# Moving the odd tokens by one partition: a TensorE matmul and a ScalarE copy in place of SyncE's DMAs

## The chip, the cores and the metric

One core of a Trainium2 chip runs the whole program. The metric is the device time of one execution in microseconds, the median of several runs. The profile is taken from one execution, and its times are counted from the start of its span.

## What is computed

A metaformer block on x of shape (4, 64, 32, 32). First a layer norm over channels, a deformable 3x3 convolution (offsets and masks from another 3x3 convolution, four corners gathered for each tap), batch norm, SiLU, and the residual sum. Then a token mixer over T = 1024 tokens of 64 channels: a layer norm of each token, K = 16 causal filters of full length, two mixing matrices for each filter, and a short autoregressive part of three lags; the weighted sum of four branches, each on a prefix of the tokens.

```
x = x + _L0_conv_ref(_ln_c(x), ...)
t = _to_tokens(x)
t = t + _L0_ffn_ref(_ln_t(t), ...)      # _stu of four prefixes, weighted
...
U_plus = irfft(Vf * rfft(u)); U_minus = irfft(Vf * rfft(u * sgn)) * sgn
out = einsum('btkd,k,kde->bte', U_plus, s, Mpp) + einsum('btkd,k,kde->bte', U_minus, s, Mpm)
```

U_plus and U_minus together are convolutions between tokens of even and of odd place, so the kernel keeps the two apart.

## The kernel before

The four images go as two pairs (bp = 0, 1). A pair's 1024 tokens are cut into NJ = 4 units of 128 even and 128 odd tokens, so there are NQ = 8 units, each with one pass n = 0 to 7; bp, j = divmod(n, 4). Tokens lie on partitions in reverse order.

VectorE makes the tokens. For each unit q and parity p it waits for the gathered corners, weighs them (weigh(q, p, b2): L459, L460, and L463, which writes V), TensorE transposes V (turn_values, L838 and L839) and convolves it (convolve_values, L848; turn_convolved), ScalarE takes the exponential (L654), and VectorE activates and normalises (finish(q, p), from L471), ending with two writes to u16 at L493 and L494 which raise u_ready. u16[:, q, hl, b, w, c] holds in slot w = 1 the even and in slot w = 0 the odd tokens as a high and a low f16 part (hl), for two images b.

Its order in time is: weigh(q, 1, 0), weigh(q, 1, 1), positions and weights of unit q + 2, finish(q, 0), weigh(q+1, 0, 0), finish(q, 1), weigh(q+1, 0, 1), and on to q + 1. V has one buffer for each image (b2), so a V write waits until TensorE's turn_values has read the last one. POOL issues the gathers, nine (one a tap) for each of the four (p, b2) of a unit, into one buffer each (L279).

TensorE runs pass n as 16 steps k. convolve(i) multiplies the filters of group i // 4 with tokens: par = i % 2 picks slots 0 and 1 or slots 1 and 2 of u16, and the result goes to conv_ps[par], one PSUM bank each. It does 3 matmuls for each unit j2 = 0 to j of the pair; only the last three, j2 = j, need the new unit. ScalarE copies each result out (L680, two copies). After convolve(k) come, each at its own k, turn_pass(n - 1) (k = 1, L876), turn_tokens(2n + 1) (k = 3, L859), turn_values for the next unit (k = 3 and 11), convolve_values (4 and 12), turn_convolved (5 and 13), turn_tokens(2n + 2) (k = 10, L859, which needs the even tokens of unit n + 1), and from k = 4 the mixing of an earlier filter (mix, L919).

Slot 2 of u16 has to hold the odd tokens moved by one partition: partition s takes slot 0 of partition s + 1, and the last partition takes partition 0 of the unit before (zero for the first unit of a pair). Before the change SyncE does this with DMAs from SBUF to SBUF, L257 for 127 partitions and L259 for the last one, 14 in all. TensorE waits for them in convolve(1) ahead of its last three matmuls (L899).

Of the kernel before, what the change touches and what calls it, by code (L numbers as in the profile page):

```python
# [5 lines left out]
F32, F16, I32 = mybir.dt.float32, mybir.dt.float16, mybir.dt.int32  # L6
ALU, ACT, AX = mybir.AluOpType, mybir.ActivationFunctionType, mybir.AxisListType

P = 128
B, C, H, W = 4, 64, 32, 32  # L10
T = H * W
BP = B // 2
NJ = T // (2 * P)
NQ = BP * NJ
# [12 lines left out]
STEPS = 4 * N_GROUPS  # L27
# [5 lines left out]
START = 2  # L33
# [14 lines left out]
def metaformer_kernel(nc, x, offset_w, offset_b, mask_w, mask_b, weight, gamma, beta, mean, var,  # L48
                      sigma, phi, m_u, m_plus, m_minus, log_weights, gumbel, ident_in, grid_in, first_row_in, out):
    ctx = ExitStack()  # L50
    with ctx:
        def sb(name, shape, dt=F32):
            return ctx.enter_context(nc.sbuf_tensor(name, shape, dt))

        def sem(name):
            return ctx.enter_context(nc.semaphore(name))
# [14 lines left out]
        ident, swap = ident_swap[:, 0, :], ident_swap[:, 1, :]  # L71
# [3 lines left out]
        zeros = sb("zeros", [C, 2 * C])  # L75
        ones = sb("ones", [K, P])
        off_bias = sb("off_bias", [P, NOFF])
        w_off = sb("w_off", [P, TAPS, NCH])
        w_scaled = sb("w_scaled", [C, TAPS * C])
        w_main = sb("w_main", [P, 5, C])  # L80
# [26 lines left out]
        u16 = sb("u16", [P, NQ, 2, 2, 3, C], F16)  # L107
# [74 lines left out]
        filt_loaded = [sem(f"filt_loaded{k}") for k in range(K)]  # L182
        conv_done = [sem(f"conv_done{i}") for i in range(2)]
        conv_copied = [sem(f"conv_copied{i}") for i in range(2)]
        shift_zeroed, u_shifted, mix_scaled = sem("shift_zeroed"), sem("u_shifted"), sem("mix_scaled")
        group_mixed, mixed_copied, pass_turned = sem("group_mixed"), sem("mixed_copied"), sem("pass_turned")
        out_copied, out_stored = sem("out_copied"), [sem(f"out_stored{i}") for i in range(2)]
        dve_step = sem("dve_step")
# [19 lines left out]
        @block.sync  # L208
        def _(sp):
            sp.dma_start(x_ch[:, 0, :], ap(x, 0, [[T, P], [1, T]])).then_inc(s_x[0], 16)  # L210
            sp.dma_start(ident_swap[:], ident_in).then_inc(s_ident, 16)
            sp.dma_start(w_off_raw[0:2 * TAPS, :], ap(offset_w, 0, [[C * TAPS, 2 * TAPS], [1, C * TAPS]])).then_inc(s_woff, 16)
            sp.dma_start(w_off_raw[2 * TAPS:NOFF, :], ap(mask_w, 0, [[C * TAPS, TAPS], [1, C * TAPS]])).then_inc(s_woff, 16)
            sp.dma_start(grid[:], grid_in).then_inc(s_const, 16)
            sp.dma_start(first_row[:], first_row_in).then_inc(s_const, 16)
            sp.dma_start(off_bias[:, 0:2 * TAPS], ap(offset_b, 0, [[0, P], [1, 2 * TAPS]])).then_inc(s_const, 16)
            sp.dma_start(off_bias[:, 2 * TAPS:NOFF], ap(mask_b, 0, [[0, P], [1, TAPS]])).then_inc(s_const, 16)
            sp.dma_start(phi_sb, ap(phi, 0, [[2 * K, P], [2 * P * K, NJ], [1, 2 * K]]).rearrange("s j (p k) -> s j p k", p=2)
                         ).then_inc(s_phi, 16)
            sp.dma_start(x_ch[:, 1, :], ap(x, 2 * C * T, [[T, P], [1, T]])).then_inc(s_x[1], 16)  # L220

            sp.wait_ge(zeroed, 1)
            for bp in range(BP):
                for first in (2 * C, 2 * C * (1 + H * W) + C):
                    sp.dma_start(ap(table[bp], first, [[IMAGE * 2 * C, 2], [2 * C, W], [1, C]]), zeros[:, 0:C]
                                 ).then_inc(border_stored, 16)
                sp.dma_start(ap(table[bp], 0, [[IMAGE * 2 * C, 3], [1, 2 * C]]), zeros[0:3, :]).then_inc(border_stored, 16)
            load_matrices(sp, 0, m_plus, range(BRANCHES))
            store_image(sp, 0, 0, 0)
            store_image(sp, 0, 1, 0)  # L230
            load_matrices(sp, 1, m_minus, range(2, BRANCHES))
            for r in range(BRANCHES):
                sp.dma_start(mu_raw[:, r, :].rearrange("d (i e) -> d i e", i=3),
                             ap(m_u, r * 3 * C * C, [[C, C], [C * C, 3], [1, C]])).then_inc(s_mats, 16)
            sp.wait_ge(f_rows_ready, 1)
            sp.dma_start(ap(hankel, 0, [[4 * HROW, K], [1, 4 * HROW]]), f_rows.rearrange("k p h c -> k (p h c)")
                         ).then_inc(f_rows_stored, 16)
            for b2 in range(2):
                for cy in range(2):
                    store_image(sp, 1, b2, cy)  # L240

            def load_filters(ks):
                for k in ks:
                    sp.dma_start(filt_h[:, k].rearrange("s p h c -> s (p h) c"),
                                 ap(hankel, k * 4 * HROW + HPAD - 2 - (P - 1), [[1, P], [HROW, 4], [1, HLEN]])
                                 ).then_inc(filt_loaded[k], 16)

            sp.wait_ge(f_rows_stored, 16)
            load_filters(range(8))
            sp.wait_ge(mats_summed, 2 * BRANCHES)  # L250
            sp.wait_ge(off_turned, 2 * BP)
            sp.wait_ge(w_ready, 2)
            load_filters(range(8, K))
            sp.wait_ge(shift_zeroed, BP)
            for q in range(NQ):
                sp.wait_ge(u_ready, 2 * q + 2)
                sp.dma_start(u16[0:P - 1, q, :, :, 2], u16[1:P, q, :, :, 0]).then_inc(u_shifted, 16)  # L257
                if q % NJ:
                    sp.dma_start(u16[P - 1:P, q, :, :, 2], u16[0:1, q - 1, :, :, 0]).then_inc(u_shifted, 16)  # L259

        @block.gpsimd
        def _(pool):
# [22 lines left out]
        def _(dve):  # L285
# [19 lines left out]
            dve.memset(ones[:], 1.0).then_inc(ones_ready, 1)  # L305
            dve.memset(roots[:, 0, 0:C], 1.0).then_inc(roots_set, 1)
            dve.memset(f_rows, 0.0)
            for q in range(0, NQ, NJ):
                dve.memset(u16[3 * P // 4:P, q, :, :, 2], 0.0).then_inc(shift_zeroed, 1)

            def reverse_pixels(bp):
                dve.wait_ge(s_x[bp], 16)
# [1 line left out]

            reverse_pixels(0)

            dve.wait_ge(s_woff, 32)
            raw = w_off_raw.rearrange("o (c t) -> o t c", t=TAPS)
            dve.tensor_copy(w_off_dup[:, :, 0, :], raw)
# [243 lines left out]
        def _(act):  # L563
# [119 lines left out]
            def store_pass(n):  # L683

                act.wait_ge(pass_turned, n + 1)
                if n >= 2:
# [4 lines left out]
                act.dma_start(ap(out, (n // NJ) * 2 * C * T + 2 * P * (n % NJ), [[T, P], [1, 2 * P]]),  # L691
                              o_sb[:, n % 2, :]).then_inc(out_stored[n % 2], 16)

            for n in range(NQ):
                for k in range(K):
                    copy_products(n, k)
                    if k == ODD_TOKENS_AT:
                        copy_tokens(2 * n + 1)
                    if n and k == 1:
                        store_pass(n - 1)  # L700
                    if n == NQ - 1:
                        continue
                    for p, (values_at, y_at, turn_at) in enumerate(HOSTED_AT):
                        r = 2 * n + 2 + p
                        if k == values_at:
                            copy_values(r)
                        if k == y_at:
                            copy_convolved(r)
                        if k == turn_at:
                            exp_y(r)  # L710
                    if k == TOKENS_AT:
                        copy_tokens(2 * n + 2)
                act.wait_ge(group_mixed, N_GROUPS * (n + 1))
                act.copy(mixed[:], acc_ps[n % 2][:, 0:2 * P].rearrange("e (b a) -> e b a", b=2)).then_inc(mixed_copied, 1)
# [5 lines left out]
        def _(pe):  # L720
# [139 lines left out]

            pe.wait_ge(w_copied, 1)
            pe.wait_ge(ones_ready, 2)
            for r in range(2):
                turn_values(r)
                convolve_values(r)
                turn_convolved(r)
# [13 lines left out]
            for n in range(NQ):  # L880
# [4 lines left out]
                ranges = [(s, max(SEGS[s][0], P * j) - P * j, min(SEGS[s][1], P * j + P) - P * j)  # L885
                          for s in range(seg0, seg0 + nseg)]

                def convolve(i):

                    g, b2, par = i // 4, i // 2 % 2, i % 2  # L890
                    if n == 0 and i % 4 == 0:
                        for k in range(GROUP * g, GROUP * g + GROUP):
                            pe.wait_ge(filt_loaded[k], 16)
                    pe.wait_ge(conv_copied[par], START + STEPS * n + 2 * (i // 2))
                    for j2 in range(j + 1):
                        if j2 == j and i == 0:
                            pe.wait_ge(u_ready, 2 * n + 2)
                        if j2 == j and i == 1:
                            pe.wait_ge(u_shifted, 16 * (7 * bp + 2 * j + 1))  # L899
                        lag = P * (j - j2)  # L900
                        for e, (hl, part) in enumerate(((0, 0), (0, 1), (1, 0))):
                            last = pe.matmul(conv_ps[par][:].rearrange("c (k a) -> c k a", k=GROUP),  # L902
                                             u16[:, NJ * bp + j2, hl, b2, par:par + 2].rearrange("s w c -> s (w c)"),
                                             filt_h[:, GROUP * g:GROUP * g + GROUP, par, part, lag + 2:lag + 2 + P],
                                             start=(j2 == 0 and e == 0), stop=(j2 == j and e == 2))
                    last.then_inc(conv_done[par], 1)
# [110 lines left out]
```

## Time and profile before

| | |
|---|---|
| median of 3 runs | 545.5 us (543.98 to 546.7) |
| the profiled execution | 545.57 us, span 543.4 us |
| mean granted clock of TensorE | 0.899 |
| PE busy | 439.2 us, 81% |
| VectorE busy | 316.9 us, 58% |
| ScalarE busy | 206.4 us, 38% |
| POOL busy | 296.8 us, 55% |

The difference of some 2 us between an execution's time and its span lies around the profiled work. Busy shares are means over the start (until about 110 us), in which filters, matrices and the first tokens are made, and the eight passes of TensorE, which follow one another to the end.

### The profile page before, as it was taken

The numbers are of one execution on the slowest core, as the hardware profiler recorded it, in microseconds if no ns is written. First come the engines' busy times: TensorE is split into PE (matmuls) and PEld (weight loads), VectorE is DVE, ScalarE is ACT, GpSimd is POOL, SyncE is SP. The second block draws the span as 40 slices with busy tenths as digits, with TensorE's granted clock in tenths as the row PEclk, the third lists the DMA queues.
The fourth block names the chain that finished last, engine by engine and source line by source line (L and its number), as shares of the span: only waits on it lengthen the run. The fifth ranks groups of instructions, "written<-read, shape, count | busy, mean of one in ns | idle before, by whom it ended". The sixth has DMA issues, their size and how long they took to land.

```text
span 543.4 us, 7147 instructions
## 1 busy us (share of the span) xinstructions
PE 439.2 (81%) x2660; PEld 217.9 (40%) x2660; DVE 316.9 (58%) x768; ACT 206.4 (38%) x413; POOL 296.8 (55%) x295
## 2 busy tenths in 40 slices
PE   4986481438775995999989996976699699989997
PEld 3442441315443442444434342643344354534333
DVE  5759977999864959292738429677374934040000
ACT  2124120125543562434333343654356244424232
POOL 1067777778777777777777773777776000000000
PEclk9999595558897999799989998889699889999999
DMA  6943699832334333333333332333433000000000
GB/s 154 185 109 106 155 326 349 259 111 83 102 102 112 102 98 109 103 104 103 104 109 98 104 100 53 104 93 108 114 103 97 6 10 1 2 5 11 0 1 10
DMA packets 47746, 54.41 MB, mean 100 GB/s; under 512 B 28656, under 2 KB 38134, under 8 KB 47713
## 3 DMA queue, kind: packets, MB, share of 16 engines
q0 software_dynamic: 13824, 37.77, 23.6%
q1 hardware_dynamic: 27865, 13.94, 10.2%
q10 hardware_dynamic: 6024, 2.26, 1.9%
q8 instruction: 21, 0.34, 0.3%
q14 instruction: 12, 0.10, 0.1%
HBM read 50.12 MB, written 3.30 MB: 98 GB/s over the span
## 4 chain that ended last, share of the span: by engine, by line
PE 58%; DVE 24%; DMA 10%; issue 3%; ACT 2%; SPq 1%; DVEq 0%
PE bank L902 32%; DMA u<-u 9%; PE bank L919 7%; PE bank L848 3%; PE bank L779 3%; DVE G L459 3%; PE bank L838 3%; DVE sil L472 2%; PE bank L760 2%; DVE G L460 2%; PE bank L939 2%; PE bank L876 1%; DMA filt<-in_L_ffn_phi_dram 1%; DVE V L463 1%; DVE st L299 1%
## 5 line engine op out<-in xcount | busy, mean ns | idle before, releaser
L279 POOL DMA_INDIRECT G<-corner_table,idx x288 | 294.2, 1022 | 122.0 <-issue 86.2
L902 PE MATMUL bank<-filt,u 128*128 128x512 f16 x960 | 243.2, 397 | 46.5 <-DMA u<-u 38.4
L680 ACT COPY u_conv<-bank 64x512 f32<-64x512 f32 x256 | 148.3, 579 | 202.7 <-PE bank L902 198.7
L902 PEld LDWEIGHTS bank<-filt,u 128*128 128x128 f16 x960 | 89.5, 100 | 167.8 <-issue 49.9
L919 PE MATMUL bank<-u_conv,mixw 128*64 128x256 f32 (+1 forms) x640 | 79.2, 356 | 5.9 <-issue 5.9
L459 DVE TENSOR_TENSOR G<-G,bank 128x2304 f32<-128x2304 f32 x32 | 81.5, 2547 | 1.3 <-DMA G<-corner_table,idx 1.2
L463 DVE TENSOR_TENSOR V<-G 128x576 f32<-128x576 f32 x32 | 24.4, 761 | 67.9 <-PE bank L839 67.2
L919 PEld LDWEIGHTS bank<-u_conv,mixw 128*64 128x64 f32 x640 | 35.8, 137 | 52.1 <-issue 50.6
L460 DVE TENSOR_TENSOR G<-G 128x1152 f32<-128x1152 f32 x32 | 43.5, 1358 | 1.1
L471 DVE TENSOR_SCALAR expo<-expo 128x128 f32<-128x128 f32 x16 | 4.4, 274 | 59.4 <-ACT expo L654 59.1
L838 PE MATMUL bank<-ident_swap,V 128*128 128x128 f32 x128 | 22.3, 309 | 14.6 <-DVE V L463 12.1
L644 ACT COPY vT<-bank 128x512 f32<-128x512 f32 x32 | 17.2, 592 | 25.5 <-PE bank L839 25.4
L848 PE MATMUL bank<-vT,w_main 128*64 128x128 f32 (+1 forms) x320 | 22.6, 292 | 3.6 <-ACT vT L645 3.6
L838 PEld LDWEIGHTS bank<-ident_swap,V 128*128 128x128 f32 x128 | 17.1, 160 | 17.8 <-issue 17.6
L848 PEld LDWEIGHTS bank<-vT,w_main 128*64 128x64 f32 (+1 forms) x320 | 20.2, 148 | 6.3 <-issue 4.9
L760 PE MATMUL bank<-ident_swap,n_uT 128*64 128x128 f32 x64 | 10.7, 361 | 12.1 <-DVE n_uT L343 12.1
L779 PE MATMUL bank<-filt,w_off 64*32 64x512 f32 x144 | 18.1, 646 | 0.0
L600 ACT COPY filt<-bank 64x256 f32<-64x256 f32 x16 | 5.4, 394 | 27.0 <-PE bank L760 27.0
L472 DVE RECIPROCAL sil<-expo 128x128 f32<-128x128 f32 x16 | 15.2, 953 | 0.5
L760 PEld LDWEIGHTS bank<-ident_swap,n_uT 128*64 128x64 f32 x64 | 10.0, 192 | 13.0 <-DVE n_uT L343 12.4
L859 PE MATMUL bank<-ident_swap,u_tok 128*128 128x128 f32 x32 | 7.4, 316 | 6.4 <-DVE u L494 6.4
L939 PE MATMUL bank<-n_uT,mu 64*64 64x256 f32 (+1 forms) x120 | 12.2, 339 | 0.0
(153 smaller groups left out, 308.5 us busy)
## 6 DMA issues: line engine op xcount, KB each, us to landing
filt<-filter_rows SPq DMA_DIRECT2D x16, 514.0 KB, 12.2
G<-corner_table,idx POOLq DMA_INDIRECT x288
corner_table<-n_uT SPq DMA_DIRECT2D x12, 128.0 KB, 3.5
mixw<-in_x_dram SPq DMA_DIRECT2D x2, 512.0 KB, 6.3
filt<-in_L_ffn_M_phi_plus_dram SPq DMA_DIRECT2D x4, 256.0 KB, 7.5
out_dram<-o_sb ACTq DMA_DIRECT2D x8, 128.0 KB, 2.0
filt<-n_L_ffn_M_phi_minus_dram ACTq DMA_DIRECT2D x2, 256.0 KB, 5.6
corner_table<-n_uT ACTq DMA_DIRECT2D x4, 128.0 KB, 4.8
```

Of the source, the lines that this page charges most:

```text
L279: pool.indirect_dma_start(G[:, k, tap, :], None, corners[bp], bass.IndirectOffsetOnAxis(ap=idx[:, q % 2, k, tap:tap + 1], axis=0)).then_in ...
L459: link(dve.tensor_tensor(g, g, w, ALU.mult))
L460: link(dve.tensor_tensor(G[:, k, :, 0:2 * C], G[:, k, :, 0:2 * C], G[:, k, :, 2 * C:4 * C], ALU.add))
L463: dve.tensor_tensor(V[:, b2].rearrange("s (t c) -> s t c", c=C), G[:, k, :, 0:C], G[:, k, :, C:2 * C], ALU.add).then_inc(v_ready[b2], 1)
L472: link(dve.reciprocal(sil[:], expo[:]))
L680: act.copy(u_conv[C * par:C * par + C, g % 2, :, b2, p, :], conv_ps[par][rows].rearrange("c (k a) -> c k a", k=GROUP)).then_inc(conv_copie ...
L760: last = pe.matmul(bank[2 + jj][C * b2:C * b2 + C, 256 * p + P * (1 - j2):256 * p + P * (1 - j2) + P], n_tok[:, NJ * bp + NJ - 1 - 2 * jj ...
L779: last = pe.matmul(bank[b2][group:group + NCH, :], w_off[half, tap, :], a, start=(t == 0), stop=(tap == TAP_HALVES[tg][-1]))
L838: pe.transpose(val_ps[b2][:, P * m:P * m + P], V[:, b2, P * m:P * m + P], ident)
L848: last = pe.matmul(y_chan_ps[C * b2:C * b2 + C, :], w_main[0:rows, m, :], vT[0:rows, b2, m, :], start=(m == 0), stop=(m == 4))
L902: last = pe.matmul(conv_ps[par][:].rearrange("c (k a) -> c k a", k=GROUP), u16[:, NJ * bp + j2, hl, b2, par:par + 2].rearrange("s w c -> s ...
L919: last = pe.matmul(acc[C * p:C * p + C, 0:2 * P].rearrange("e (b a) -> e b a", b=2)[:, :, a0:a1], mixw[:, s, C * k:C * k + C], u_conv[:, g ...
```

## The change

The DMAs and the memsets of slot 2 go. VectorE writes a "ladder" of 128 x 256 in f16 at the start: the identity with zeros left and right of it. In each pass TensorE multiplies slot 0 of the new unit by a slice of the ladder that moves it by one partition, and, for j > 0, adds partition 0 of the unit before by a second matmul. The result goes to conv_ps[1], of which ScalarE copies 256 columns to slot 2. convolve(1) waits for this copy ahead of its first matmul.

```diff
+        ladder = sb("ladder", [P, 2 * P], F16)
...
-            sp.wait_ge(shift_zeroed, BP)
-            for q in range(NQ):
-                sp.wait_ge(u_ready, 2 * q + 2)
-                sp.dma_start(u16[0:P - 1, q, :, :, 2], u16[1:P, q, :, :, 0]).then_inc(u_shifted, 16)
-                if q % NJ:
-                    sp.dma_start(u16[P - 1:P, q, :, :, 2], u16[0:1, q - 1, :, :, 0]).then_inc(u_shifted, 16)
...
-            for q in range(0, NQ, NJ):
-                dve.memset(u16[3 * P // 4:P, q, :, :, 2], 0.0).then_inc(shift_zeroed, 1)
+            dve.memset(ladder[:, 0:P - 1], 0.0)
+            dve.memset(ladder[:, 2 * P - 1:2 * P], 0.0)
...
+            dve.wait_ge(s_ident, 16)
+            dve.tensor_copy(ladder[:, P - 1:2 * P - 1], ident).then_inc(ladder_ready, 1)
...
+            def copy_stepped(n):
+
+                act.wait_ge(u_stepped, n + 1)
+                act.copy(u16[:, n, :, :, 2], conv_ps[1][:, 0:4 * C].rearrange("s (h b c) -> s h b c", h=2, b=2)).then_inc(u_shifted, 1)
+
             for n in range(NQ):
+                copy_stepped(n)
                 for k in range(K):
                     copy_products(n, k)
...
+            pe.wait_ge(ladder_ready, 1)
...
+                def step_odd_tokens():
+
+                    pe.wait_ge(u_ready, 2 * n + 2)
+                    pe.wait_ge(conv_copied[1], START + STEPS * n)
+                    dst = conv_ps[1][:, 0:4 * C].rearrange("s (h b c) -> s h b c", h=2, b=2)
+                    last = pe.matmul(dst, ladder[:, P:2 * P], u16[:, n, :, :, 0], start=True, stop=(j == 0))
+                    if j:
+                        last = pe.matmul(dst, ladder[:, 0:P], u16[:, n - 1, :, :, 0], start=False, stop=True)
+                    last.then_inc(u_stepped, 1)
+
...
                     for j2 in range(j + 1):
                         if j2 == j and i == 0:
-                            pe.wait_ge(u_ready, 2 * n + 2)
-                        if j2 == j and i == 1:
-                            pe.wait_ge(u_shifted, 16 * (7 * bp + 2 * j + 1))
+                            step_odd_tokens()
+                        if j2 == 0 and i == 1:
+                            pe.wait_ge(u_shifted, n + 1)
```

## Rows read from the trace of the kernel before

**Rows 1.** The page: shares of the chain that ended last, and the convolution's group.

```profile
PE bank L902 32%; DMA u<-u 9%; PE bank L919 7%; PE bank L848 3%; PE bank L779 3%; DVE G L459 3%; PE bank L838 3%; DVE sil L472 2%; PE bank L760 2%; DVE G L460 2%; PE bank L939 2%; PE bank L876 1%; DMA filt<-in_L_ffn_phi_dram 1%; DVE V L463 1%; DVE st L299 1%
...
L902 PE MATMUL bank<-filt,u 128*128 128x512 f16 x960 | 243.2, 397 | 46.5 <-DMA u<-u 38.4
```

**Rows 2.** The waits: engine and line, whom for, us in total, times, longest.

```profile
POOL G L279 <- DVE V L463: 9.1, 4, 7.8
```

**Rows 3.** Timeline of TensorE, pass 2: start, us, work, [idle before <- releaser].

```profile
208.37 3.43 PE L902 MATMUL bank<-filt,u 128*128 128x512 f16 x15
217.87 1.46 PE L902 MATMUL bank<-filt,u 128*128 128x512 f16 x3 [6.08 <-DMA u<-u]
219.26 1.12 PE L876 MATMUL bank<-mixed,ident_swap 128*64 128x128 f32 x8
220.32 5.58 PE L902 MATMUL bank<-filt,u 128*128 128x512 f16 x18
```

**Rows 4.** Windows: pass 0; then first matmul or tokens to k = 3, passes 1-3, 5-7.

```profile
core 0: us, PE busy (x) PEld busy (x) DVE busy (x) ACT busy (x) POOL busy (x), PEclk, DMA share, GB/s
110.18:143.60 33.42, 20.68 (x148) 10.98 (x148) 31.66 (x73) 14.89 (x28) 26.11 (x25) 0.79 0.33 98
160.12:174.34 14.22, 6.96 (x29) 2.87 (x30) 8.43 (x5) 3.78 (x7) 11.17 (x11) 0.76 0.40 111
208.37:225.73 17.36, 11.28 (x46) 4.59 (x44) 9.07 (x8) 4.02 (x8) 13.40 (x14) 0.80 0.38 109
267.58:282.91 15.33, 12.67 (x58) 5.39 (x56) 7.80 (x5) 4.02 (x8) 11.98 (x12) 0.89 0.39 108
376.28:391.56 15.28, 8.16 (x30) 3.16 (x30) 8.34 (x5) 3.87 (x7) 11.93 (x12) 0.66 0.42 112
425.58:440.71 15.13, 11.34 (x46) 4.58 (x44) 8.91 (x7) 4.02 (x8) 0.00 (x0) 0.77 0.06 14
482.56:495.03 12.47, 11.30 (x59) 4.95 (x56) 0.00 (x0) 4.02 (x8) 0.00 (x0) 1.00 0.06 16
```

**Rows 5.** Timeline of TensorE, pass 7, after its wait.

```profile
488.45 0.82 PE L902 MATMUL bank<-filt,u 128*128 128x512 f16 x3 [1.17 <-DMA u<-u]
489.21 0.66 PE L876 MATMUL bank<-mixed,ident_swap 128*64 128x128 f32 x8
489.80 5.39 PE L902 MATMUL bank<-filt,u 128*128 128x512 f16 x24
```

**Rows 6.** Timeline of VectorE, passes 1, 2 and 4.

```profile
165.91 2.55 DVE L459 TENSOR_TENSOR G<-G,bank 128x2304 f32<-128x2304 f32 x1 [1.20 <-DMA G<-corner_table,idx]
...
176.68 2.54 DVE L459 TENSOR_TENSOR G<-G,bank 128x2304 f32<-128x2304 f32 x1
...
227.99 2.55 DVE L459 TENSOR_TENSOR G<-G,bank 128x2304 f32<-128x2304 f32 x1
...
344.14 0.78 DVE L463 TENSOR_TENSOR V<-G 128x576 f32<-128x576 f32 x1 [4.89 <-PE bank L839]
```

**Rows 7.** Timeline of ScalarE at the seam of passes 1 and 2.

```profile
208.15 0.37 ACT L714 COPY mixed<-bank 128x256 f32<-128x256 f32 x1 [2.08 <-PE bank L919]
210.58 1.19 ACT L680 COPY u_conv<-bank 64x512 f32<-64x512 f32 x2 [2.06 <-PE bank L902]
```

**Rows 8.** Timeline of POOL: the ninth gathers of (2, 2), (2, 3) and (3, 3).

```profile
161.24 0.95 POOL L279 DMA_INDIRECT G<-corner_table,idx  x1 [0.31 <-issue]
...
173.47 0.94 POOL L279 DMA_INDIRECT G<-corner_table,idx  x1 [0.30 <-issue]
...
221.24 0.95 POOL L279 DMA_INDIRECT G<-corner_table,idx  x1 [0.30 <-issue]
```

**Rows 9.** Timeline of TensorE: the token turn at k = 10, passes 1, 2, 4.

```profile
192.71 0.49 PE L859 MATMUL bank<-ident_swap,u_tok 128*128 128x128 f32 x2
...
248.66 0.49 PE L859 MATMUL bank<-ident_swap,u_tok 128*128 128x128 f32 x2
...
359.62 0.54 PE L859 MATMUL bank<-ident_swap,u_tok 128*128 128x128 f32 x2 [2.61 <-DVE u L494]
```

**Rows 10.** The chain in order of time, pass 2: start, us, what.

```profile
209.86 7.96 DMA u<-u
```

More of the change, by code:

```diff
@@ L184, in metaformer_kernel @@
         conv_copied = [sem(f"conv_copied{i}") for i in range(2)]
-        shift_zeroed, u_shifted, mix_scaled = sem("shift_zeroed"), sem("u_shifted"), sem("mix_scaled")
+        ladder_ready, u_stepped, u_shifted, mix_scaled = sem("ladder_ready"), sem("u_stepped"), sem("u_shifted"), sem("mix_scaled")
         group_mixed, mixed_copied, pass_turned = sem("group_mixed"), sem("mixed_copied"), sem("pass_turned")
```

## The prediction

> **What bounds the kernel now.** I read the page first. The convolution line L902 has 46.5 us of idle time in front of it, 38.4 us of that put down to the DMA u<-u, and in the chain of waits u<-u is 9%, some 49 us [rows 1]. The chain counts a transfer from its issue, while TensorE still works beside part of it; so 38.4 us, the idle time, is the more honest ceiling.
>
> Then the list of waits, to see who else is short of time: POOL (the gathers) waits 9.1 us for VectorE in all four times [rows 2]. So the gathers run almost without a pause, and when TensorE gets faster, they don't.
>
> Then one pass in order of time, TensorE alone. Pass 2 (j = 2) [rows 3]: from 208.37 come 15 convolution matmuls (i = 0: 6 for old units, 3 for the new one; i = 1: 6 for old units), then 6.08 us idle until 217.87 for u<-u, the last 3 of i = 1, the 8 of turn_pass, and the 18 of i = 2 and 3. The reader should see two losses: the idle time, and the pace after it: 0.49 us a matmul, then 0.31, where pass 7 does 24 in 5.39, 0.22 each [rows 5]. The windows of the same stretch in every pass say why [rows 4]: granted clock 0.66 to 0.89 in passes 1 to 6, 1.00 in pass 7, whose wait was only 1.17 us [rows 5]. The two levels are 1.2 and 2.4 GHz: TensorE idle for several us came back at 1.2.
>
> **The change part by part.** *Start.* Two memsets of u16 go; two memsets and one 128x128 copy for the ladder come, on VectorE, while it waits for the weights' DMAs. Without that cover they cost at most the 0.78 us of a 128x576 write [rows 6]; I take 0.
>
> *Removed.* Fourteen DMAs on SP's queue; nothing is queued behind them there. *Added on TensorE.* One or two matmuls of 256 columns a pass; at 0.22 us for 512 that is 0.22 us for two. *Added on ScalarE.* One 128x256 copy a pass; the one of that size that ends a pass takes 0.37 us, and ScalarE is idle for 2.06 us behind it [rows 7], so nothing is pushed back. *Added wait.* convolve(1) now waits for that copy ahead of its first matmul, not only its last three, since both use conv_ps[1]. The step is done at 0.22, ScalarE starts perhaps 0.25 later (my guess), and copies for 0.37: 0.85 to 0.9 us after the tokens, and the 3 matmuls of i = 0 (0.66) cover TensorE until 0.88. I take 0.2 us of wait; bounds 0 and 1.0 (it starts late and takes the 0.6 of one of the two 64x512 copies [rows 7]). Queued behind it on TensorE are turn_pass and the whole pass, and ScalarE's copies wait for these.
>
> *A pass after.* Let A be the moment at which the tokens are there and TensorE has done the 3j old matmuls of i = 0. From A to the token turn of k = 3: (3 + 9(j+1)) matmuls at 0.22, turn_pass 0.6 as in pass 7 [rows 5], step and wait 0.42. That is 5.6, 7.6 and 9.6 us for j = 1, 2, 3. Before, the same stretch is the window of [rows 4] less 3j x 0.22 in front of A (in passes 1 and 5 the window begins at the tokens, with those done): 14.2, 16.0, 13.4, 15.3, 13.8 and 10.5 us in passes 1, 2, 3, 5, 6, 7. TensorE by itself would gain 8.6, 8.4, 3.8, 9.7, 6.2 and 0.9 us. Pass 7 gives little because the 9 old matmuls of i = 1 covered most of the DMA.
>
> *Where a gain is taken back.* At k = 10 TensorE needs the tokens of finish(n+1, 0), and VectorE makes these after weigh(n+1, 1, 1), which needs the last gather of the unit.
>
> Pass 1: that weigh started at 176.68 [rows 6]. The V before it had waited for L839, so an earlier TensorE would let it start at about 171; but the last of its nine gathers leaves POOL at 174.41 [rows 8]. For the group before, POOL was done at 162.19 and VectorE waited until 165.91, 3.7 us on, with u<-u under way; this one had landed by 176.68, at most 2.3 us on [rows 6, 8]. I take 176.2. So these tokens come 0.5 us earlier, not 8.6. VectorE had them at 191.3 (14.6 us after the weigh), and TensorE turned them at 192.71 [rows 9]. Now it is there at 184, idles 7 us until 190.8, and comes back at 1.2 GHz as after the DMA. In pass 2 that cost 2 us (18 matmuls in 5.6 for 3.9, turn_pass 1.1 for 0.6) [rows 3, 5]. 192.7 - 190.8 = 1.9 gained, 1.9 to 2 lost: pass 1 gives 0. Ends: -1 and +8.6.
>
> Pass 2: weigh(3, 1, 1) started at 227.99 behind a V that had waited for L839. POOL is done at 222.19, landing 224.2: 3.8 us earlier, tokens at 239.3 (they take 15.1 us from there). TensorE would be at k = 10 at 248.66 - 8.4 = 240.3 [rows 6, 8, 9]. It just doesn't wait; 8.4 stands. In pass 3 the gathers are 10 us ahead, in 5 and 6, carrying POOL on at its pace, by my count 3 and 6; those gains stand.
>
> Pass 0: VectorE is busy for 31.66 of 33.42 us between the two tokens, against 20.68 for TensorE [rows 4]; it sets the pace, so TensorE's wait for the DMA there (the 38.4 us holds some 6 of it) was covered: 0. Pass 4 (j = 0) is of the same kind, TensorE waiting 2.61 us at k = 10 for tokens [rows 9]. But there VectorE's own chain holds 4.89 us of waiting for L839, until 344.14 [rows 6], and with k = 3 reached earlier that is gone: 4.7 us.
>
> Sum: 0 + 0 + 8.4 + 3.8 + 4.7 + 9.7 + 6.2 + 0.9 = 33.7 us. The profiled execution took 545.57 us for a span of 543.4; the median of the runs is 545.5. 545.5 - 33.7 = 511.8, and a span of 509.7.
>
> **Two rules against the rows.** The transfers take 7.96 us in pass 2 [rows 10]. The Trainium skill, "DMA: Bandwidth & Descriptors", Anatomy of one DMA, fits 2.0 us plus bytes over 436 GB/s, an estimate of 2.2 us for these 63.5 KB; by that the old matmuls of i = 1 would hide nearly all of it and the change would give under 5 us. The row decides; why it is so long, the same page may tell (the section on the increment of 16): 127 partitions put a transfer on one DMA engine.
>
> The clock is in my sum with some 7 us over passes 2 to 6, 1.3% of the span. The Trainium skill, "TensorE: Matmul & The Clock Gate", Part 1, calls the penalty of the ramp less than 1% of a typical span, which would make this part under 5.4 us; [rows 4] show it above that.
>
> **Rivals.** *Nothing is taken back in pass 1* (VectorE's weigh moves after all, or the clock holds). Against: the rows of [rows 8] are POOL's own pace. 511.8 - 8.6 = 503. Chance 0.12.
>
> *The gathers take back pass 2 as well* (landing 3.7 us after POOL, as once seen, and the idle time costs clock): the slack is 1.0 us there, and 3 in pass 5. 511.8 + 3 to 8.4 gives 515 to 520; chance 0.17.
>
> *The clock is not won back*: TensorE idles in passes 1 and 5 for the tokens, and at each handoff, and stays at 1.2 GHz after it. Against: pass 7 stayed at 1.00 with 1.17 us of wait. 511.8 + 7 = 519; chance 0.10.
>
> *Slower*: in every pass the wait at k = 10 takes the DMA's place, as in pass 1, TensorE restarts at 1.2 GHz there, and the handoff comes on top: 0.5 us lost a pass, some 4 us in all, 549. It decides from the point at which weigh(n+1, 1, 1) can't start earlier in any pass, with gathers landing less than 1.4 us ahead of it; in pass 2 POOL is done 5.8 us ahead [rows 6, 8]. Chance 0.03.
>
> *No change*: the handoff through ScalarE lasts about as long as the DMA, over 5 us. 0.37 us and ScalarE's idle time [rows 7] speak against. 545; chance 0.02.
>
> **How the numbers follow.** My case has 0.56, and 507 to 516 by itself: handoff of 0 to 1.0 in 7 passes (-1.4 to +5.6, seldom all), start up to 0.8, pass 1 down to -1, and as much the other way for landings. With the rivals at 503 and 520 the range is 502 to 521. A measurement of this kernel tells about 0.5% (2.7 us) from no change: faster 0.95, same 0.02, slower 0.03.
>
> **What would show it.** No u<-u in the chain or the waits; eight 128x256 copies of some 0.4 us more on ScalarE, and TensorE at rest under 0.5 us for each. Granted clock near 1.0 in the stretches of [rows 4] of passes 2, 3 and 6. A new wait of some 7 us of L859 for L494 in pass 1, and pass 1 as long as before, 49 us. POOL done a few us earlier than 419, without most of its 9.1 us. I am wrong if pass 2 too has an idle stretch at k = 10, if the clock falls in spite of short waits, or if the copy starts late behind other work on ScalarE.

## The result, and the profile after

| | before | changed |
|---|---|---|
| median | 545.7 us (543.98 to 546.7, 4 runs) | 509.55 us (506.91 to 512.73, 4 runs) |
| ratio | | 0.9343, 95% interval 0.9284 to 0.9402 |
| profiled execution, span | 545.57, 543.4 us | 512.73, 510.7 us |
| mean granted clock | 0.899 | 0.916 |

The prediction was 511.8 us and a span of 509.7. The profiled execution of the changed kernel is the slowest of its four; a second profile (run 9 below) has a span of 505.9, and beside that run the kernel before had 542.72 us. So the gain is 36.2 us by the medians here, 33.7 by those of run 9.

The page, chain and costliest groups, to be held against [rows 1]:

```profile
PE bank L916 34%; POOL G L274 21%; PE bank L933 9%; PE bank L851 2%; PE bank L841 2%; DVE G L456 2%; PE bank L782 2%; PE bank L953 1%; DMA filt<-in_L_ffn_phi_dram 1%; PE bank L754 1%; DVE G L457 1%; PE bank L763 1%; PE bank L862 1%; DVE sil L469 1%; PE bank L880 1%
...
L916 PE MATMUL bank<-filt,u 128*128 128x512 f16 x960 | 235.0, 386 | 0.4 <-ACT u_conv L677 0.4
```

The transfer is gone from the chain, and the convolution's idle time fell from 46.5 to 0.4 us. Of that, 38.4 us were the wait for u<-u; the rest, 8.2 us for the tokens, is still there and stands before the step now (L897, 8.3 us). In the transfer's place in the chain stands POOL with 21%: the chain now runs back along the gathers from VectorE's weigh at 177.49 in pass 1. (L916 is L902 of before, L862 is L859, L880 is L876, L456 is L459, L460 is L463, L274 is L279.)

The waits (for whom; us in total, times, longest), against [rows 2] and the single 1.20 us of [rows 6]:

```profile
DVE G L456 <- DMA G<-corner_table,idx: 15.2, 3, 6.9
...
PE bank L862 <- DVE u L491: 12.4, 3, 6.9
...
PE bank L897 <- DVE u L491: 8.3, 3, 5.6
...
POOL G L274 <- DVE V L460: 1.2, 4, 0.3
```

And the line of before that the second one grew from:

```profile
PE bank L859 <- DVE u L494: 6.4, 2, 3.8
```

VectorE now waits for gathers, and TensorE's wait at the k = 10 turn has a third place, pass 1, beside passes 0 and 4. POOL waits 1.2 us for VectorE in place of 9.1, and its last gather ends at 414.2 in place of 419.4.

The timeline of TensorE, pass 2, against [rows 3], and of ScalarE in the same place, against [rows 7]:

```profile
211.61 0.27 PE L897 MATMUL bank<-u,ladder 128*128 128x256 f16 x1
211.72 0.27 PE L899 MATMUL bank<-u,ladder 128*128 128x256 f16 x1
211.83 2.83 PE L916 MATMUL bank<-filt,u 128*128 128x512 f16 x12
214.59 0.66 PE L880 MATMUL bank<-mixed,ident_swap 128*64 128x128 f32 x8
215.18 4.09 PE L916 MATMUL bank<-filt,u 128*128 128x512 f16 x18
219.10 0.38 PE L862 MATMUL bank<-ident_swap,u_tok 128*128 128x128 f32 x2
```

```profile
212.03 0.37 ACT L694 CAST u<-bank 128x256 f16<-128x256 f32 x1 [1.57 <-PE bank L899]
212.73 1.19 ACT L677 COPY u_conv<-bank 64x512 f32<-64x512 f32 x2 [0.34 <-PE bank L916]
```

The 3 matmuls of i = 0 and the 9 of i = 1 run as one group of 12 while ScalarE copies. From the first step matmul to turn_pass it is 2.98 us; the step takes 0.22 and 12 matmuls 2.62 at 0.218 each, so TensorE rests 0.14 us. The 18 matmuls behind turn_pass take 4.09 us, not 5.58.

The windows from the tokens or the step to the turn of k = 3, against [rows 4]:

```profile
core 0: us, PE busy (x) PEld busy (x) DVE busy (x) ACT busy (x) POOL busy (x), PEclk, DMA share, GB/s
110.42:143.79 33.37, 21.44 (x149) 11.67 (x149) 31.62 (x74) 15.28 (x29) 26.07 (x25) 0.76 0.33 96
161.02:166.93 5.91, 5.56 (x32) 2.59 (x33) 5.84 (x5) 4.14 (x8) 4.46 (x5) 1.00 0.40 115
211.61:219.10 7.49, 7.49 (x41) 3.43 (x40) 7.39 (x5) 4.25 (x8) 5.66 (x7) 1.00 0.42 114
262.91:272.36 9.45, 9.45 (x51) 4.29 (x49) 5.78 (x4) 4.26 (x8) 7.34 (x7) 1.00 0.37 111
360.75:366.30 5.55, 5.55 (x31) 2.59 (x32) 5.48 (x4) 4.15 (x8) 4.33 (x5) 1.00 0.42 124
401.63:409.13 7.50, 7.50 (x42) 3.43 (x41) 7.40 (x5) 4.25 (x8) 5.67 (x7) 1.00 0.39 114
452.93:462.38 9.45, 9.45 (x51) 4.29 (x49) 0.00 (x0) 4.25 (x8) 0.00 (x0) 1.00 0.04 14
```

The stretch was forecast at 5.6, 7.6 and 9.6 us for j = 1, 2 and 3, at full clock: it takes 5.55 to 5.6 (less the wait for the tokens' flag in pass 1), 7.5 and 9.45, and the clock reads 1.00 in all six. Pass 0 is as long as before.

Timeline of VectorE, pass 1, of POOL against [rows 8], and of TensorE at the k = 10 turns of passes 1, 2, 4, against [rows 6] and [rows 9]:

```profile
177.49 2.56 DVE L456 TENSOR_TENSOR G<-G,bank 128x2304 f32<-128x2304 f32 x1 [6.88 <-DMA G<-corner_table,idx]
```

POOL, the ninth gather of that group:

```profile
174.70 0.95 POOL L274 DMA_INDIRECT G<-corner_table,idx  x1 [0.30 <-issue]
```

TensorE:

```profile
192.21 0.80 PE L862 MATMUL bank<-ident_swap,u_tok 128*128 128x128 f32 x2 [6.85 <-DVE u L491]
192.79 2.77 PE L916 MATMUL bank<-filt,u 128*128 128x512 f16 x6
...
242.03 0.49 PE L862 MATMUL bank<-ident_swap,u_tok 128*128 128x128 f32 x2
...
344.09 0.74 PE L862 MATMUL bank<-ident_swap,u_tok 128*128 128x128 f32 x2 [2.29 <-DVE u L491]
```

In pass 1 the weigh starts at 177.49, no earlier than before (176.68). POOL is done with its ninth gather at 175.65 (174.41 before), and VectorE goes on 1.84 us after that. TensorE idles 6.85 us for what comes of it, and its next 6 matmuls take 2.77 us where the same six take 1.47 in run 3, which has no wait there.

### The profile page after: what moved, and what is told of

It is laid out like the page before. It is cut to its first block, busy times and chain, and to the rows that moved or that the text cites. A ratio compares the mean times of both kernels' runs of the same rounds, so it can differ in the third digit from the quotient of the medians.

```text
span 510.7 us, 7182 instructions
## 1 busy us (share of the span) xinstructions
PE 436.3 (85%) x2674; PEld 218.9 (43%) x2674; DVE 316.9 (62%) x769; ACT 209.9 (41%) x421; POOL 299.0 (59%) x295
## 4 chain that ended last, share of the span: by engine, by line
PE 57%; POOL 21%; DVE 10%; issue 8%; DMA 2%; ACT 1%; SPq 1%; POOLq 0%
PE bank L916 34%; POOL G L274 21%; PE bank L933 9%; PE bank L851 2%; PE bank L841 2%; DVE G L456 2%; PE bank L782 2%; PE bank L953 1%; DMA filt<-in_L_ffn_phi_dram 1%; PE bank L754 1%; DVE G L457 1%; PE bank L763 1%; PE bank L862 1%; DVE sil L469 1%; PE bank L880 1%
## 5 line engine op out<-in xcount | busy, mean ns | idle before, releaser
L274 POOL DMA_INDIRECT G<-corner_table,idx x288 | 296.4, 1029 | 114.6 <-issue 86.7
L916 PE MATMUL bank<-filt,u 128*128 128x512 f16 x960 | 235.0, 386 | 0.4 <-ACT u_conv L677 0.4
L916 PEld LDWEIGHTS bank<-filt,u 128*128 128x128 f16 x960 | 88.2, 98 | 113.7 <-issue 25.4
L456 DVE TENSOR_TENSOR G<-G,bank 128x2304 f32<-128x2304 f32 x32 | 81.5, 2548 | 15.3 <-DMA G<-corner_table,idx 15.2
L460 DVE TENSOR_TENSOR V<-G 128x576 f32<-128x576 f32 x32 | 24.4, 761 | 28.0 <-PE bank L842 27.2
L862 PE MATMUL bank<-ident_swap,u_tok 128*128 128x128 f32 x32 | 8.0, 336 | 12.4 <-DVE u L491 12.4
L763 PEld LDWEIGHTS bank<-ident_swap,n_uT 128*64 128x64 f32 x64 | 10.4, 197 | 8.2 <-DVE n_uT L340 7.6
L862 PEld LDWEIGHTS bank<-ident_swap,u_tok 128*128 128x128 f32 x32 | 6.2, 218 | 16.1 <-DVE u L491 13.3
```

The costliest lines, as they stand in the source:

```text
L274: pool.indirect_dma_start(G[:, k, tap, :], None, corners[bp], bass.IndirectOffsetOnAxis(ap=idx[:, q % 2, k, tap:tap + 1], axis=0)).then_in ...
L456: link(dve.tensor_tensor(g, g, w, ALU.mult))
L460: dve.tensor_tensor(V[:, b2].rearrange("s (t c) -> s t c", c=C), G[:, k, :, 0:C], G[:, k, :, C:2 * C], ALU.add).then_inc(v_ready[b2], 1)
L763: last = pe.matmul(bank[2 + jj][C * b2:C * b2 + C, 256 * p + P * (1 - j2):256 * p + P * (1 - j2) + P], n_tok[:, NJ * bp + NJ - 1 - 2 * jj ...
```

## The experiments

All with the kernel before run beside them on the same chip; its medians there were 542.7 to 545.3 us, and each ratio is to them. Since the first tokens come at different times in different executions (106 to 111 us, whatever the kernel), traces are compared by lengths within the passes.

**1. Fill the DMA's wait, before.** Does the low clock cost anything of its own?

```diff
                         if j2 == j and i == 1:
+                            for _ in range(WARM[n]):    # 0, 30, 25, 10, 15, 29, 15, 0
+                                pe.matmul(val_ps[0][:]..., u16[:, n, 0, b2, 0:2]..., filt_h[...], start=True, stop=True)
                             pe.wait_ge(u_shifted, 16 * (7 * bp + 2 * j + 1))
```

> The kernel before, with convolution matmuls of no use (into a bank that is free then) while TensorE waits for u<-u in passes 1 to 6: 30, 25, 10, 15, 29 and 15 of them at 0.22 us, less than the wait each time. The DMA stays. My reading (the low clock after the wait is a loss of its own, some 7 us of the sum, in passes 2, 3, 5 and 6): about 538.5 us, 0.987 of before; granted clock near 1.0 in the stretch after each wait, turn_pass 0.6 and not 1.1 us. Rival (the clock only goes with the wait and costs nothing that counts, or is given back at k = 10): 545 us, ratio 1.00.

532.12 us, ratio 0.977 (0.9713 to 0.9828): more than forecast. The windows from TensorE's restart to the turn of k = 3, passes 2, 5 and 6:

```profile
216.17:221.44 5.27, 5.27 (x30) 2.45 (x30) 0.00 (x0) 2.70 (x5) 4.05 (x5) 1.00 0.39 113
...
375.51:379.48 3.97, 3.97 (x24) 1.88 (x25) 0.00 (x0) 2.62 (x5) 3.06 (x4) 1.00 0.37 101
420.79:426.06 5.27, 5.27 (x29) 2.45 (x30) 1.80 (x2) 2.71 (x5) 0.00 (x0) 1.00 0.09 28
```

Before, the same stretches took 7.86, 6.68 and 7.92 us (restart at 217.87, 384.88 and 432.79). Over the six filled passes the stretch is 13.0 us shorter, and from TensorE's first work on the tokens on the span is 13.4 us shorter. The clock was a loss of its own, of 2.4% of the span. The two sums agree in part by chance. Pass 1 hands on only 0.5 of the 1.5 us by which its stretch is shorter, since its odd tokens came 17.5 us after k = 10 of pass 0 and not 16.4. Pass 5 gains 1.6 us more than its stretch, because the wait at k = 10 of pass 4 is 1.31 and not 2.61 us and the clock holds behind it.

**2. Cut the transfer, before.** Was the DMA the price, or its shape?

```diff
-                sp.dma_start(u16[0:P - 1, q, :, :, 2], u16[1:P, q, :, :, 0]).then_inc(u_shifted, 16)
+                sp.dma_start(u16[0:112, q, :, :, 2], u16[1:113, q, :, :, 0]).then_inc(u_shifted, 16)
+                sp.dma_start(u16[112:P - 1, q, :, :, 2], u16[113:P, q, :, :, 0]).then_inc(u_shifted, 16)
...
-                            pe.wait_ge(u_shifted, 16 * (7 * bp + 2 * j + 1))
+                            pe.wait_ge(u_shifted, 16 * (11 * bp + 3 * j + 2))
```

> The kernel before, with the DMA of 127 partitions cut into one of 112 and one of 15. One theory (the DMA is slow because of its shape, the transfer of 127 partitions runs on one engine, and the one-partition DMA sits behind it): lands in under 3 us, TensorE's wait falls from 38 us to under 10, and the time to 515 to 520, nearly the changed kernel's. Rival (every small DMA beside the gathers takes this long, and one more costs another issue of 0.7 us): 546 to 550 us, with waits as before.

515.36 us, ratio 0.9464 (0.9408 to 0.952). TensorE and SP's queue, pass 1:

```profile
163.63 0.93 PE L903 MATMUL bank<-filt,u 128*128 128x512 f16 x3 [2.42 <-DMA u<-u]
```

```profile
159.70 0.63 SPq L257 DMA_DIRECT2D u<-u  x1
160.38 0.90 SPq L258 DMA_DIRECT2D u<-u  x1
161.32 0.73 SPq L260 DMA_DIRECT2D u<-u  x1
```

TensorE goes on 3.9 us after the tokens, where it took 8.7, though there is one transfer more. The one-partition transfer holds the queue for 0.73 us; before it held it for 4.3 to 5.4. TensorE's wait for u<-u is 10.4 us in all, in place of 38.4. By the ratios to the kernel before, 5.4 of the change's 6.6% came of leaving this shape of transfer and not of leaving the DMA: about four fifths. (By the two profiles it is 29.1 of 33.0 us, but the changed kernel's is its slowest execution.)

The Trainium skill, "DMA: Bandwidth & Descriptors", the section on the increment of 16, gives a transfer of 127 partitions one DMA engine, and 112 partitions 16 by its rule. The trace agrees as far as it goes: it does not name the engines, but in pass 1 the 512 pieces of 128 bytes of both transfers go from 161.4 to 168.2, at most three under way at a time, and cut in three the same bytes go in 2.1 us, up to 19 at a time.

**3. Fewer gathers, changed kernel.** Is it the gather that takes pass 1's gain back? This kernel leaves out the ninth tap of units 1 and 2, a part of the computation: eight gathers less.

```diff
-                        for tap in range(TAPS):
+                        for tap in range(LAST_TAP[q]):    # 9, 8, 8, 9, 9, 9, 9, 9
...
-                dve.wait_ge(gathered[k], 16 * TAPS * (q + 1))
+                dve.wait_ge(gathered[k], 16 * sum(LAST_TAP[:q + 1]))
```

> The changed kernel, with the ninth tap of units 1 and 2 not gathered (the weighing takes what the buffer holds): 8 gathers fewer, 10.5 us of POOL. My reading (in pass 1 the last gather of unit 2 takes the gain back): the wait of VectorE for the gather of (2, 3), 6.9 us, goes; TensorE's wait for tokens at k = 10 of pass 1 falls from 6.9 to under 1, its clock holds, and the time goes from 509.6 to 500 or 501. Rival (VectorE's own work sets the tokens of k = 10): 508 to 510.

Median 502.4 us, ratio 0.9238 (0.9168 to 0.9308). Of its six executions one took 847.61 us, for a reason that nothing here shows; it is in the median and not in the ratio. The others lie between 496.44 and 503.37, and the profiled one is of the short ones. In its profile VectorE weighs without a pause in pass 1, and TensorE does not wait at k = 10:

```profile
179.88 0.49 PE L863 MATMUL bank<-ident_swap,u_tok 128*128 128x128 f32 x2
180.21 1.47 PE L917 MATMUL bank<-filt,u 128*128 128x512 f16 x6
```

From k = 10 of pass 0 to k = 10 of pass 1 it is 40.3 us, against 48.4: the 8.1 us that the gather had taken in the profile shown (5.6 against that of run 9). By the medians the gathers left out are worth 7 us.

**4. The late token turn, changed kernel.** TOKENS_AT = 14 in place of 10.

> The changed kernel, with turn_tokens(2n+2) at k = 14 and not 10, so that TensorE can do the values of k = 11 to 13 before it waits for the even tokens of the next unit. If the chain at k = 10 (tokens, values, activation, odd tokens) sets passes 0, 1 and 4: VectorE starts finish(n+1, 1) 5 us earlier in passes 0 and 4 and up to 7 in pass 1, capped by the gather for unit 3 in pass 2 (tokens of k = 10 there at 239.7 as now); 8 us by the start of pass 3 and 5 in pass 4: 496 to 498 us. Rival (VectorE and the gathers set these passes whatever TensorE's order): 508 to 510.

498.43 us, ratio 0.9168 (0.9106 to 0.9229). From step to step, passes 0, 1 and 4 are 6.1, 3.6 and 4.4 us shorter than in the profile of the changed kernel; pass 5 is 0.7 longer, and the others are as they were. Against the profile of run 9 the three are 6.1, 0.2 and 2.8: in pass 1 most of the gain is the spread between executions. The waits:

```profile
DVE G L456 <- DMA G<-corner_table,idx: 53.6, 11, 6.8
```

VectorE now waits for gathers eleven times: POOL sets the pace of the short passes. The reason holds for passes 0 and 4 that TensorE, standing at k = 10 for even tokens, kept VectorE from the odd ones.

**5. Fill the wait at k = 10, changed kernel.** 14, 30 and 9 matmuls of no use ahead of turn_tokens(2n + 2) in passes 0, 1 and 4.

> The changed kernel, with convolution matmuls of no use ahead of the token turn at k = 10: 14 in pass 0, 30 in pass 1, 9 in pass 4, each lot shorter than the wait there. If the low clock after that wait is the second half of what is taken back: from the turn at k = 10 of pass 1 to the step of pass 2 takes 17.0 us (as before the change) and not 19.4, and passes 0 and 4 give 1.0 to 1.5 each; 504 to 505 us. Rival (VectorE's chain behind k = 13 sets the tokens anyway): 509.

507.64 us, ratio 0.9352 (0.9303 to 0.9401). In the trace from k = 10 of pass 1 to the step of pass 2 it is 16.97 us, against 19.40. Against the profile shown passes 0, 1 and 4 are 6.7 us shorter by the steps, but against the second profile (run 9) only 1.7; the medians say 1.4 to 1.9. Behind the two waits of 6.85 and 4.30 us it cost 2.4 and 1.6 us. The mechanism is there, but 504 to 505 us was too much to expect; its size in a usual execution is below what the times can tell.

**6. A longer handoff, changed kernel.**

```diff
+                act.copy(spare[:, n], conv_ps[1][:, 0:4 * C])
                 act.copy(u16[:, n, :, :, 2], conv_ps[1][...]).then_inc(u_shifted, 1)
```

> The changed kernel, with a second copy of the stepped tokens (to a tile that nobody reads) ahead of the one that counts, so that the handoff takes 0.37 to 0.4 us longer in each pass. If the copy is just covered by the three matmuls of i = 0: turn_pass comes about 0.4 us later after the step in each pass, and 7 passes make 2 to 3 us: 511.5 to 512.5. If the cover had room: no change, 509.6. If the handoff is a long one that I misread: over 514.

510.49 us, ratio 0.9377 (0.9326 to 0.9427), not to be told from the changed kernel by time, and less than forecast. TensorE, pass 2:

```profile
211.27 0.81 PE L918 MATMUL bank<-filt,u 128*128 128x512 f16 x3
212.26 2.11 PE L918 MATMUL bank<-filt,u 128*128 128x512 f16 x9 [0.17 <-ACT u L696]
```

From step to turn_pass it is 3.25 us in place of 2.98, and 0.26 to 0.28 more in each of the seven passes; the copies follow each other at 0.27. What one adds to the handoff comes out in full in the trace: the cover by 3 matmuls was just used up.

**7. Cut transfer and late turn, before.** Runs 2 and 4 together, with DMAs.

> The kernel before with the transfer cut into 112 and 15 partitions and turn_tokens(2n+2) at k = 14. If what is left of the DMA (some 2 us of wait at j = 1, 1.2 to 1.8 at j = 2) is on the path in every pass, as in the run of the cut transfer alone: 4 us above the changed kernel with the late token turn, 502. Rival (with the late turn the gathers set the pace of the short passes and cover the DMA): 499 to 500.

505.03 us, ratio 0.9284 (0.9237 to 0.9331). TensorE still waits 10.8 us for u<-u in six places. With the late turn the matmul and the copy are better than the well-shaped DMA by 1.2% (0.9168 against 0.9284, whose intervals just part), some 6 us and not the 4 that I gave; the gathers don't cover it.

**8. All together, changed kernel.** Late turn, the step's result in the bank of the turned values, old matmuls of convolve(1) first.

```diff
-                    dst = conv_ps[1][:, 0:4 * C]...
+                    dst = val_ps[1][:, 0:4 * C]...
...
+                    if i == 0:
+                        pe.wait_ge(conv_copied[1], START + STEPS * n)
+                        for j2 in range(j):
+                            multiply(1, j2)
+                        step_odd_tokens()
+                    if i == 1:
+                        pe.wait_ge(u_shifted, n + 1)
+                    last = multiply(i, j)
```

> The changed kernel with turn_tokens(2n+2) at k = 14, the step's result in the bank of the turned values (free at that time), and all matmuls of convolve(1) for old units ahead of the wait for the odd tokens; convolve(1) waits for ScalarE's copy only ahead of its last three. By my reading the handoff costs TensorE only 0.15 us a pass, and the old matmuls cover 0.65 us of the waits for tokens in passes 1 and 5: 1.5 to 2.5 us under the late turn alone, 496 to 497. Rival (the shared bank cost the change a lot): under 494. Rival (the gathers set the pace now): 498.5.

498.89 us, ratio 0.918 (0.9144 to 0.9216): the same as run 4. My 496 to 497 was wrong and the rival with the gathers was right; VectorE waits for them 12 times, 48.7 us. Taking the handoff off the shared bank buys nothing here.

**9. The changed kernel again.**

> The changed kernel once more, without an edit, for a second profile beside the one shown. What every execution should share: a rest of 0.15 us between step and old matmuls of i = 1, a gather that VectorE waits 6 to 7 us for in pass 1, TensorE's wait of 6 to 7 us at k = 10 there. What may differ, if the moment at which the clock rises again is not tied to the program: the stretches behind the waits of passes 0, 1 and 4, by 1 to 2.5 us each, so that spans lie between 504 and 511. Rival (these stretches are the same each time): a span within 0.5 us of 510.7, start apart.

509.02 us, ratio 0.9382 (0.9344 to 0.9419), span 505.9. By the steps, passes 2, 3, 5, 6 and 7 are the same to 0.01 us; pass 1 takes 46.88 us against 50.24, and pass 4 37.15 against 38.73. VectorE's wait for the gather in pass 1:

```profile
175.07 2.55 DVE L456 TENSOR_TENSOR G<-G,bank 128x2304 f32<-128x2304 f32 x1 [4.30 <-DMA G<-corner_table,idx]
```

And POOL, the ninth gather of that group:

```profile
172.35 0.95 POOL L274 DMA_INDIRECT G<-corner_table,idx  x1 [0.30 <-issue]
```

VectorE goes on 1.77 us after this gather has left POOL, 1.84 in the first profile. My "6 to 7 us in every execution" was wrong, and what varies is POOL, not the landing: it comes to its 108th gather at 172.35 in one execution and at 174.70 in the other (173.47 in the kernel before). Up to there 10, 12 and 11 of its gathers took 1.3 to 2.0 us in place of 0.95.

Pass 4 differs for another reason. TensorE waits there as long in both, 2.31 us and 2.29, and then runs at full clock in one and at half in the other:

```profile
340.89 0.49 PE L862 MATMUL bank<-ident_swap,u_tok 128*128 128x128 f32 x2 [2.31 <-DVE u L491]
341.22 0.81 PE L916 MATMUL bank<-filt,u 128*128 128x512 f16 x3
```

In the first profile the same three matmuls, at 344.63, take 1.49 us. The mean clock from k = 10 of pass 4 to the step is 1.00 here and 0.90 there, and the stretch 15.08 and 16.66 us.

**10. Without the one-partition transfers, before.**

> The kernel before without the one-partition DMAs (partition 127 of slot 2 stays zero in all units: that part of the computation is left out). In pass 4, which has none, TensorE went on 6.5 us after the tokens; in passes 1, 2, 3 and 5 it took 8.0 to 8.8, in 6 and 7 6.7. If the one-partition DMA waits behind the other and adds its own: 6.0 to 6.5 us in all passes, 2 us less wait in four passes, 538 to 541. Rival (the transfer of 127 partitions alone sets it, pass 4 was short by chance): waits and time as before, 545.

538.98 us, ratio 0.9928 (0.9903 to 0.9953). Partition 127 is left at zero here. The time is the one forecast, the waits are not: TensorE goes on 7.4 to 7.9 us after the tokens in passes 1 to 5 (8.7 before in passes 1 and 5). Pass 4 is among them with 7.5, where it had 6.6 before. So the big transfer alone is nearly all of the wait, and pass 4 had not been short for want of the other one. In passes 6 and 7, when the gathers are over, it is 6.5. The 4 us come to a good part from the clock: in pass 3 the wait is down to 2.12 us, the clock reads 1.00 behind it, and the stretch takes 6.57 us in place of 7.95; in passes 2 and 6 it is 6.85 and 6.90 in place of 7.86 and 7.92.

```profile
271.29 0.82 PE L900 MATMUL bank<-filt,u 128*128 128x512 f16 x3 [2.12 <-DMA u<-u]
```

**11. Late turn, before.**

> The kernel before, DMAs and all, with turn_tokens(2n+2) at k = 14. If the token turn at k = 10 is the lock in passes 0 and 4 whatever moves the odd tokens: 5 us in each of these and nothing in the others, where TensorE hardly waited at k = 10: 535. If it pays only once the DMA's wait is gone: 543 to 545.

530.41 us, ratio 0.9783 (0.9732 to 0.9834): 12 us, no less than on the changed kernel (0.9343 to 0.9168 is 10) and more than forecast. Within the noise the two changes add up.

## Why the prediction was right, point by point

The token turns at k = 10 divide the run. Gains from one to the next, predicted and measured, with the profile before (turns at 143.62, 192.71, 248.66, 310.40, 359.62, 409.92, 463.63) against the first of the changed kernel (143.79, 192.21, 242.03, 299.85, 344.09, 384.66, 432.05) and against that of run 9:

| stretch that ends at | predicted | measured | by run 9 |
|---|---|---|---|
| k = 10 of pass 0, from the tokens | 0 | 0.1 | 0.1 |
| k = 10 of pass 1 | 1.9 | 0.7 | 3.2 |
| k = 10 of pass 2 (8.4 less 1.9 for the clock) | 6.5 | 6.1 | 6.9 |
| k = 10 of pass 3 | 3.8 | 3.9 | 3.9 |
| k = 10 of pass 4 | 4.7 | 5.0 | 5.0 |
| k = 10 of pass 5 | 9.7 | 9.7 | 11.3 |
| k = 10 of pass 6 | 6.2 | 6.3 | 6.3 |
| the end | 0.9 | 1.1 | 1.1 |
| sum | 33.7 | 32.9 | 37.9 |

That the sum is met within 0.8 us is in part luck: the first profile is the slowest of four. In another execution passes 1, 2 and 5 gave 5 us more, for two things that the prediction held fixed, the moment at which POOL comes to a gather and the clock behind a wait.

*The ceiling.* 38.4 us of idle time was called the ceiling, and it was none: the low clock behind the idle time comes on top, 13.0 us by run 1. The sum did not rest on it. It was made from the windows, and these gave passes 3, 6 and 7 within 0.2 us in both profiles, and pass 5 in the first.

*The handoff.* 0.2 us of wait taken, 0.14 to 0.16 measured. The guess of 0.25 us for ScalarE's start was 0.2 (TensorE goes on behind the step at 211.83, the copy starts at 212.03). Run 6 shows that there was no room left. ScalarE's eight copies took 0.37 us each.

*Pass 1 gives nothing.* The mechanism was as said, and run 3 gives the 8.1 us back. The landing was well sized: 1.8 us after POOL taken, 1.84 and 1.77 measured. What was off is POOL, taken to be done at 174.41 as before: it was done at 175.65 in one execution and at 173.30 in the other. So the weigh came at 177.49 and 175.07 for the 176.2 forecast. And the odd tokens of pass 1 came 17.5 us after k = 10 of pass 0 in both profiles, not 16.4 as in the kernel before. The change didn't do this: runs 1, 2 and 10, which leave the DMA in, have 17.5 too; the profile before had the shorter one. It is the clock: the mean was 0.83 and 0.86 in this stretch, 0.90 before, and run 5, which fills the wait of 3.25 us in front of it, takes 15.0.

*Pass 2 stays clear.* It did, by less than it looks: no wait at 242.03, and VectorE waited 3.85 us for gather (3, 3).

*Passes 0 and 4.* VectorE's chain set them, as said, but for a reason that I did not see: the order at k = 10. Run 4 takes 6.1 us out of pass 0 and 4.4 or 2.8 out of pass 4, by the profile that it is held against.

*The clock.* The term was mis-sized. I put it at some 7 us; run 1 measures 13.0. I left out the three matmuls right behind the wait (0.64 us in each of six passes), pass 1 (1.5 with them) and pass 4 (2.2). The sum did not suffer, since it was made from whole windows and not from idle time plus clock. The Trainium skill, "TensorE: Matmul & The Clock Gate", Part 1, puts the penalty of the ramp at less than 1% of a typical span; run 1 measures 2.4% here.

*The DMA's price.* The fit that the prediction takes from the Trainium skill, "DMA: Bandwidth & Descriptors", Anatomy of one DMA, stands there for transfers that GpSimd issues. SyncE issues these, so it was no rule against the rows to begin with.

*The rivals.* "Nothing taken back in pass 1" is what run 3 makes, 8 us less in pass 1. "Taken back in pass 2 as well" didn't come in either profile. "The clock is not won back" is refuted by 1.00 in all six windows. "Slower" needed a wait at k = 10 in every pass: there is one in passes 0, 1 and 4. "No change" needed a handoff of 5 us: the copy ends 0.8 us after the step begins.

What stays open: why some of POOL's gathers take 1.3 to 2.0 us, more of them in one execution than in another, and why the clock falls behind a wait of 2.29 us and not behind one of 2.31.

## What to carry to other kernels

Cut the run at fixed points of the program and cost each stretch as a whole, at the pace that the same matmuls have where nothing waits; idle time and a low clock behind it are then counted once. Ask of every gain which queue doesn't get faster with it: here the gathers, with a pace of 1.25 us each, took one pass back, and a turn that stood too early in TensorE's order cost more (10 to 12 us) than all that was left in the handoff. Before a DMA is replaced, try another shape of it: two transfers in place of one gave four fifths of the gain. And hold a forecast against more than one profile: two of the same kernel differed by 4.8 us.

## What the runs showed of the hardware

A transfer of 127 partitions (508 pieces of 128 bytes) between two places of SBUF held TensorE until 8.7 us after the tokens in pass 1, 7.8 without the one-partition DMA behind it; as 112 and 15 partitions it was 3.9. The one-partition DMA held SP's queue for 4.3 to 5.4 us behind the whole transfer, for 0.7 behind the cut ones. Its pieces and those of the transfer in front of it went at most three at a time, those of the cut ones up to 19.

Behind the six waits for u<-u of 2.66 to 7.26 us of the kernel before (passes 1 to 6) TensorE came back at 1.2 GHz; behind 1.17 us (pass 7), 1.34 us (pass 5 after) and 2.12 us (pass 3 of run 10) it came back at 2.4. In between it was either: at k = 10 of pass 4 it came back at 1.2 GHz behind 2.29 us and at 2.4 behind 2.31 (run 9) and 2.33 (run 2). With the six waits filled with matmuls of no use the stretches behind them took 13.0 us less in all.

VectorE went on 1.7 to 2.3 us after the ninth gather of a group had left POOL, in all eight of its waits for gathers in the two profiles of the changed kernel. POOL gave out a gather each 1.25 us, and now and then took up to 1.1 us longer for one.

The same program on the same inputs had spans of 510.7 and 505.9 us with five of eight passes equal to 0.01 us; nearly all the difference lay in two passes in which TensorE waits for VectorE, in one by POOL's pace and the clock behind it (3.4 us), in the other by the clock alone (1.6 us).
